# A count matrix built one chunk and one block at a time, in PSUM banks picked by registers, with W_in folded and the degrees summed from slabs

## The reference

```python
h = x @ W_in + b_in                        # x: relu(layernorm(x))
deg = segment_sum(ones, dst); deg = maximum(deg, 1.0)
for l in range(3):
    agg = segment_sum(h[src], dst) / deg
    h = relu(agg @ W_agg[l] + h @ W_self[l] + b_hid[l])
return h @ W_out + b_out
```

## Time and profile before

| | us |
|---|---|
| median of 3 runs | 7475.61 |
| lowest and highest | 7471.18, 7477.4 |
| profiled execution, span | 7482.7 |
| PE, DVE, ACT, POOL busy | 6524.4, 3687.6, 2350.1, 3090.6 |
| mean granted clock of PE | 0.929 of 2.4 GHz |

### The profile page before, as it was taken

How to read it: one execution, slowest core, us unless ns; L and a number is a source line. 1 busy time by engine, 2 the same in 40 slices (tenths; PEclk the granted TensorE clock), 3 DMA queues, 4 the chain that set the end, 5 groups by cost and what they waited for, 6 DMA issues and landing times.

```text
span 7482.7 us, 126299 instructions
## 1 busy us (share of the span) xinstructions
PE 6524.4 (87%) x29550; PEld 4866.3 (65%) x29551; DVE 3687.6 (49%) x10588; ACT 2350.1 (31%) x6423; POOL 3090.6 (41%) x3455
## 2 busy tenths in 40 slices
PE   5888888999999999998888987599999997777777
PEld 2333333788877878776666666477778886666666
DVE  9999999111111112224777777612223333555554
ACT  6888887000000001112222221312223333222222
POOL 5777776000100011114777775200011111777775
PEclk9999999999999999998877777799999998899898
DMA  5555557877987797775333333688897775444443
GB/s 194 211 215 211 214 213 250 316 273 274 336 292 272 280 339 260 253 255 173 101 99 99 99 99 103 234 324 290 294 357 245 249 246 188 119 122 121 121 123 95
DMA packets 668862, 1601.14 MB, mean 214 GB/s; under 512 B 77659, under 2 KB 306989, under 8 KB 668605
## 3 DMA queue, kind: packets, MB, share of 16 engines
q1 hardware_dynamic: 543133, 1232.09, 46.5%
q0 software_dynamic: 125488, 365.75, 16.1%
HBM read 1208.17 MB, written 390.27 MB: 214 GB/s over the span
## 4 chain that ended last, share of the span: by engine, by line
PE 51%; POOL 11%; issue 7%; DMA 7%; DVE 4%; ACT 1%; DVEq 1%; SPq 0%; POOLq 0%; ACTq 0%
PE psum L1343 35%; POOL ring L1096 6%; PE psum L1192 4%; PE psum L1619 3%; POOL tbuf L1096 3%; PE psum L1591 2%; DMA g_own<-own_dram 2%; POOL rb L1096 2%; DMA slab<-adj 2%; PE psum L1603 1%; PE psum L1522 1%; PE psum L1187 1%; PE psum L1292 1%; PE psum L1301 1%; DMA tbuf<-rel_table,idx_slot 1%
## 5 line engine op out<-in xcount | busy, mean ns | idle before, releaser
L1343 PE MATMUL psum<-X,slab 128*128 128x512 f32 x12495 | 3104.2, 402 | 87.8 <-DMA slab<-adj 43.7
L1343 PEld LDWEIGHTS psum<-X,slab 128*128 128x128 f32 x12495 | 2345.2, 190 | 618.7 <-DVE g_x L2336 89.3
L2486 DVE TENSOR_TENSOR acc<-acc,psum 128x264 f32 (+1 forms) x1660 | 704.2, 424 | 508.1 <-PE psum L1619 369.1
L1008 POOL DMA_DIRECT2D table<-s_tab x147 | 80.2, 545 | 1905.2 <-DVE s_tab L2083 1905.2
L974 POOL TENSOR_SCALAR hot_j<-iota_j,col_now 128x392 bf16<-128x392 bf16 x587 | 783.3, 1346 | 0.0
L1464 PE MATMUL psum<-hot_j,hot_key 128*128 128x392 bf16 x2348 | 583.6, 330 | 190.5 <-DVE hot_j L2299 149.0
L2313 DVE SCALAR_TENSOR_TENSOR staged<-staged,keep_all,psum 128x392 fp32r<-128x392 f32 x1174 | 717.0, 611 | 7.6 <-PE psum L1464 5.2
L1706 ACT ACTIVATE key_sq<-iota_row,edge_key 128x128 f32<-128x128 f32 x2055 | 657.4, 389 | 2.3 <-DVE staged L2288 2.3
L2083 DVE TENSOR_TENSOR s_tab<-psum,s_tab 128x256 fp32r<-128x256 f32 x196 | 82.7, 422 | 1141.5 <-ACT s_tab L1663 1141.5
L2299 DVE TENSOR_SCALAR hot_j<-iota_j,edge_col 128x392 bf16<-128x392 bf16 x1761 | 567.3, 349 | 0.0
L1658 ACT COPY s_hT<-psum 128x256 f32<-128x256 f32 x273 | 101.7, 373 | 1349.2 <-PE psum L1187 1349.2
(11 more groups left out here) (417 smaller groups left out, 8822.3 us busy)
## 6 DMA issues: line engine op xcount, KB each, us to landing
slab<-adj SPq DMA_DIRECT2D x385, 1344.0 KB, 6.5
slab<-adj SPq DMA_DIRECT2D x315, 896.0 KB, 5.9
adj<-staged SPq DMA_DIRECT2D x1174, 196.0 KB, 1.9
X<-table SPq DMA_DIRECT2D x33, 1792.0 KB, 13.0
table<-s_tab POOLq DMA_DIRECT2D x147, 256.0 KB, 3.1
g_own<-own_dram POOLq DMA_DIRECT2D x35, 896.0 KB, 8.4
own_dram<-s_out POOLq DMA_DIRECT2D x147, 128.0 KB, 5.5
acc<-zero_rows SPq DMA_DIRECT2D x2, 6600.0 KB, 27.4
```

The source lines that it names most:

```text
L1343: last = nc.tensor.matmul(sums_of(j), slab[:, slab_at(c), u, j * P:(j + 1) * P], X[:, x_at(p, d), :], start=(d == 0), stop=(d == KT - 1))
L2486: V.tensor_tensor(a, a, psum[:, bank, 0:w], ALU.add).then_inc(sem("summed"), 1)
```

## The change

The chunks are now single (782 of 128 edges), a step is the meeting of one chunk with one block, and a block with many chunks is cut after every 32: 1592 steps, 808 parts. PE accumulates a part in one bank of a ring of four, picked by a register z (its running number + 1), and clears the next bank with a two-column matmul in each step, after waiting until it has been evicted. ACT evicts each part once, when the step count of its end, read from a register, is reached; SP stores it. DVE makes all hot columns and the even keys, POOL the odd ones. Where z and the ends come from: DVE computes them at the start, POOL scatters the ends by 13 indirect DMAs (parts_dram), SP reads them back. x is loaded whole (49 tiles) and its statistics are taken before the build. W_in is multiplied into the agg and self weights by PE at the start, its bias likewise. The degrees: DVE adds up all rows of each group's slabs one group ahead, PE turns the sum into columns with seven one-column matmuls, and SP waits for DVE (slab_summed) too before it fills a slab's buffer. Early slabs and rows of pass 0 are issued by POOL.

```diff
-    C2 = C // 2
-    MEETS = C2 + BLOCKS - 1
-    PART = 16
-    BUILD = 24
+    PART = 32
+    CUTS = (C - 1) // PART
+    ENDED = BLOCKS + CUTS
+    RING = 4
+    LEAD = RING - 1
+    BUILD = 32
+    HOT, KEYS = 16, 32
+    NOW = 16
+    MEETS = -(-(C + BLOCKS - 1 + CUTS) // AT_ONCE) * AT_ONCE
...
             def slab_in(p, k, c, i=None):
                     sp.wait_ge(*ev("slab_done", at if i is None else i * NC + at))
+                    if p == 0 or p == 1 and k == 0 and c < SLABS:
+                        sp.wait_ge(*ev("slab_summed", at if i is None else i * NC + at))
...
+            def parts_out(i):
+                sp.load(to_regs, part_to[0:1, bass.ds(i * AT_ONCE, AT_ONCE)])
+                for r in range(AT_ONCE):
+                    sp.wait_ge(*ev("evicted", i * AT_ONCE + (LEAD + r + 1)))
+                    to = sp.snap(to_regs[r], min_val=0, max_val=PARTS + MORE - 1)
...
+            for s in range(SB2):
+                nc.gpsimd.indirect_dma_start(
+                    out=parts_dram, out_offset=bass.IndirectOffsetOnAxis(ap=at_i[:, s:s + 1], axis=0),
+                    in_=part_out[:, s, :], in_offset=None).then_inc(sem("parts_stored"), 16)
...
+            def group_degrees(slabs):
+                def f(t0):
+                    pe.wait_ge(*ev("slab_summed", slabs))
+                    pe.wait_ge(*ev("l0_own", t0 + 1))
+                    for j in range(GT):
+                        last = nc.tensor.matmul(PS_DEG[:, j:j + 1], slab_sum[:, j * P:(j + 1) * P], ones[:, 0:1], start=True, stop=True)
+                    last.then_inc(sem("l0_degrees"), GT)
...
+            def cleared(bank_ap):
+                nc.tensor.matmul(bank_ap, iota_k[:], iota_k[:, 0:2], start=True, stop=True, skip_group_check=True)
             def build(t, steps):
                 for s in range(steps):
                     beside(in_stages, t, s)
-                    for h in range(2):
-                        last = nc.tensor.matmul(psum[:, s % 4, 0:J], hot_key[:, s // 2 % 4, s % 2, h, :], ...
-                    last.then_inc(sem("meet_mm"), 1)
-                    if not static or n >= 2:
-                        degrees(t, s - 2)
+                    if s % AT_ONCE == 0:
+                        pe.load(zs, step_part[0:1, bass.ds(t * BUILD + s, AT_ONCE)])
+                    z = pe.snap(zs[s % AT_ONCE], min_val=1, max_val=LEAD + ENDED)
+                    if s % 4 == 0:
+                        pe.wait_ge(*ev("hot", t * BUILD + (s + 4)))
+                        pe.wait_ge(*ev("hot_odd", t * (BUILD // 2) + (s // 2 + 2)))
+                    own = (z & (RING - 1)).with_bounds(min_val=0, max_val=RING - 1)
+                    nc.tensor.matmul(psum[:, bass.ds(own, 1), 0:J].rearrange("p o j -> p (o j)"), hot_key[:, s % KEYS, :], hot_j[:, s % HOT, :],
+                                     start=False, stop=True, skip_group_check=True).then_inc(sem("meet_mm"), 1)
+                    pe.wait_ge(sem("evicted"), z)
+                    next_own = ((z + 1) & (RING - 1)).with_bounds(min_val=0, max_val=RING - 1)
+                    cleared(psum[:, bass.ds(next_own, 1), J:J + 2].rearrange("p o j -> p (o j)"))
...
+            def parts_evicted(i):
+                act.load(last_regs, part_last[0:1, bass.ds(i * AT_ONCE, AT_ONCE)])
+                for r in range(AT_ONCE):
+                    act.wait_ge(sem("meet_mm"), act.snap(last_regs[r], min_val=1, max_val=MEETS))
+                    if not isinstance(i, int):
+                        act.wait_ge(*ev(f"staged_out{r}", i * 16))
+                    nc.scalar.copy(staged[:, r, :], psum[:, (r + 1) % RING, 0:J]).then_inc(sem("evicted"), 1)
...
+            dve.wait_ge(*ev("in_x", 16 * X_LOADS))
+            for t in range(T):
+                last = V.bn_stats(x_st[:, t, :], x_all[:, t, :])
...
             def hot_columns(s):
+                if s % 2 == 0:
+                    V.tensor_scalar(hot_key[:, s % KEYS, :], iota_k[:], edge_now[:, 1, s:s + 1], None, op0=ALU.is_equal)
+                V.tensor_scalar(hot_j[:, s % HOT, :], iota_j[:], edge_now[:, 0, s:s + 1], None, op0=ALU.is_equal).then_inc(sem("hot"), 1)
...
-                    V.scalar_tensor_tensor(out=staged[:, s % AT_ONCE, :], in0=staged[:, (s - 1) % AT_ONCE, :].bitcast(F32), ...
+            def slabs_summed(g, i, c):
+                for u in range(2 if c == 0 else 0, SIZES[c]):
+                    V.tensor_tensor(slab_sum, slab_sum, of[u], ALU.add).then_inc(sem("slab_summed" if u == SIZES[c] - 1 else "slab_partly"), 1)
...
+            dve.wait_ge(*ev("meet_mm", MEETS))
+            for c in range(NC):
+                slabs_summed(0, None, c)
+                if c == 6:
+                    gathered_rows()
+                if c == 12:
+                    turn_tables()
```

More of the change, by code:

```diff
@@ L278, in build @@
         X_FIRST = 2
[L279 removed]
+        X_EARLY = 3
+        X_AT = [[n * GT for n in range(NG)],
                 [2 * GT, 3 * GT, 4 * GT, 5 * GT, 6 * GT, 0, GT]]
@@ L508, in tiles_of, with early @@
             return tile
+        EARLY = [(17, "rows", 0), (31, "rows", 1), (35, "slab", 0), (37, "slab", 1), (39, "slab", 2), (41, "slab", 3), (45, "rows", 2)]
+        def early(name, n):
+            return next(16 * (at + 1) for at, (_, *what) in enumerate(EARLY) if what == [name, n])
+        for n in range(SLABS):
+            shared[f"slab{n}"] = (f"slab_in{n}", -16)
         def x_in(p, b):
@@ new lines, in _ @@
+            last.then_inc(sem("in_WB"), 1)
+            pe.wait_ge(*ev("in_WT_read", 1))
+            for n, name in enumerate(("agg", "self")):
+                for q in range(Q):
+                    for b in range(Q):
+                        last = nc.tensor.matmul(PS_W[n][:, q * D:(q + 1) * D], s_u[:, b, q, :], cols(W["in", name], D)(b),
+                                                start=(b == 0), stop=(b == Q - 1))
+                last.then_inc(sem("in_W"), 1)
+            pe.wait_ge(*ev("bound", 1))
@@ L1486, in _ @@
+            by_meets(pe, build, 2)
+            pe.wait_ge(*ev("evicted", LEAD + ENDED))
             pe.wait_ge(*ev("in_own", T + 1))
@@ new lines, in _ @@
+            bounds_read(bounds_t, "bound_read")
+            once(V.tensor_scalar(to2, block, float(BLOCKS), float(MORE), op0=ALU.is_ge, op1=ALU.mult))
+            once(V.tensor_tensor(to2, to2, block, ALU.add))
+            once(V.tensor_scalar(other, to2, -1.0, float(BLOCKS - 1), op0=ALU.mult, op1=ALU.add))
+            once(V.tensor_tensor(other, other, cuts, ALU.mult))
+            once(V.tensor_tensor(to2, to2, other, ALU.add))
+            once(V.tensor_scalar(at2, step, float(ELSEWHERE), None, op0=ALU.add))
@@ L2193, in _ @@
+            once(V.tensor_tensor(at2, at2, upto, ALU.add))
+            V.tensor_copy(at_i, at2)
+            once(V.scalar_tensor_tensor(out=code, in0=code, scalar=before[:, 0:1], in1=cuts, op0=ALU.add, op1=ALU.mult))
             once(V.tensor_tensor(to2, to2, code, ALU.add))
+            V.tensor_copy(part_out[:, :, 0], to2)
+            V.tensor_scalar(part_out[:, :, 1], step, 1.0, None, op0=ALU.add).then_inc(sem("parts_out"), 1)
             once(V.tensor_scalar(code, code, 1.0, None, op0=ALU.subtract))
```

780 lines of the change are left out of this document (384 added, 396 removed), and 2 rows, old and new, of the table TILE_EVENTS.

## The result

The changed kernel takes 7602.18 us (median of 4 runs, 7597.29 to 7607.17) where the kernel before takes 7476.5: a ratio of 1.0166, 95% interval 1.0152 to 1.0181. It is slower by about 125 us. They stand in four places: the first matmul of the build comes 15.5 us later, the build is 71.5 us longer, pass 0 is 29.6 us longer, and all the rest is 6 us.

The account below looks back on a forecast made before the run. It took PE's own queue of register operations to bound the new build, where DVE had bound the old. Terms of 37 + 12 + 24 = +73 us on 7475.6 gave 7549 us, with a range of 7340 to 7680.

Parts of the forecast that it names:

- the likeliest case: Build on PE: six register operations a step, step 0.77 to 0.83 us, total 7500 to 7630; chance 0.46.
- The queue bounds the build: Build: PE's register operations, 0.106 us each and six a step, set the pace; the other engines cost nothing beside PE.
- Term 1: Build: 1592 steps of 0.796 us give 1267 us against 1230 before, +37 us.
- Term 2: Start, DVE's chain before the first step: +12 us, mostly the layer norm's statistics of 49 tiles, about +18.
- Term 3: Pass 0, slab sums on DVE and one-column products on PE: +24 us, from +10 to +70.
- one-column products: Pass 0: seven more PE products per group for the degrees, 1.4 us a group, 10 us in all.
- The ring of slabs: Pass 0: a slab is freed only when DVE and PE have read it; 1 to 1.5 us per group, 9 us.
- The first group: Pass 0: DVE waits for the last edge transposes with slabs unsummed, about 5 us for PE.
- The rest: The other passes and both edge stages stay as they were.
- Five operations a step: Build: copy of z free or one mask fused; step 0.690, build 1098 us, total 7380; chance 0.26.
- The queue free of bounds and DVE at 0.42: Build: PE's queue isn't the bound, DVE's 0.42 us is the step; build 669, total 6950; chance 0.05.
- Loads by SP's price: Build: register loads cost PE what SP pays, 0.20 us more a step, total 7860; dearer load or wait, chance 0.08.

Follow-up runs that it names:

- load_four: Changed kernel with TensorE loading four registers every fourth step in place of eight every eighth: 7630.4 us in one run.
- short_stats: Changed kernel with the 49 statistics at the start reading 16 of 256 columns: 7601.63 us in one run.
- two experiments on pass 0: Changed kernel with, in one, DVE's slab sums cut to 8 columns (7615.65 us); in the other, one PE degree product per group in place of seven (7593.8 us).
- act_zeroed: Changed kernel without clearing matmuls: ScalarE zeroes each bank after copying it out, and PE has two register operations a step; ratio 0.9678 to the kernel before.
- narrow_columns: Changed kernel with VectorE's hot columns compared over 8 columns in place of 392 in the loop's turns: 7609.04 us in one run.
- wide_clear: Changed kernel with each step's clearing matmul writing 120 columns in place of 2: 7617.11 us, ratio 1.0173 to the kernel before.
- short_sums: Changed kernel with VectorE's slab sums in pass 0 adding 8 columns in place of 896 from each group's third row on: 7615.65 us.
- one_degree: Changed kernel with TensorE making one one-column product per group of pass 0 in place of seven: 7593.8 us.
- seven_ops: Changed kernel with one mask more in each step, seven register operations in place of six: 7748.88 us in one run.
- five_ops: Changed kernel without the copy of z into a second register, five register operations a step in place of six: 7507.48 us.
- four_ops: Changed kernel with both banks packed into the loaded word, so four register operations a step and no copy: 7387.57 us, ratio 0.9877 to the kernel before.
- four_ops_wide: The kernel of four_ops with the clearing matmul widened from 2 to 120 columns: ratio 0.9833 to the kernel before.
- zero_narrow: The kernel of act_zeroed with ScalarE zeroing 8 columns of a part's bank in place of 392: 7143.28 us in one run.

## Why the prediction was right, and where its terms were off

The direction, and the mechanism of the likeliest case, held; 7549 was forecast and 7602 measured, inside the range and inside the narrower 7500 to 7630 of the likeliest case. The three terms and the rest all erred the same way, by 34.5, 3.5, 5.6 and 6 us. Point by point:

**The queue bounds the build: shown.** Six operations, each 0.106 forecast and 0.087 to 0.104 found (without the 0.03 of a matmul, which the forecast had in it); 0.636 forecast for a plain step, 0.64 found. Adding one costs 161 us, leaving one or two out gives 86 and 206. DVE, ACT, SP and POOL were rightly costed at nothing.

**Term 1 was +71.5, not +37; what was mis-sized is the load.** The prediction took 0.35 us for a load of eight registers from a row of four words in 0.332. The row was right (load_four repeats it at 0.333), but eight are 0.593 at the median and 0.72 on the mean, up to 2.11, and the next operation starts 0.06 after a load's end: 0.78 from start to start. Why 82 of the 199 last longer than 0.61 is open; a queue still full of matmuls isn't the reason, for the load at 613.21 us lasts 1.09 although the last matmul before it ended 0.05 us after its start. With its address a load is 0.106 a step where 0.057 stood: 0.049 x 1592 = 78 us. Two smaller errors took nearly as much off, 0.044 a step or 70 us: the waits of every fourth step cost 0.024, since one of the two is carried by the mask and needs no instruction, and not 0.053; loop and layer 0.035 and not 0.05. The six operations with their matmuls are 0.654 over all steps and not 0.636, 29 us more. Sum 0.819, measured 0.818. That term 1 was off by only 34 us is in part luck.

**Term 2 was +15.5, not +12.** The statistics took 16.1 us of DVE (18 forecast) and short_stats shows them on the path. 2.4 us of it came back at the end of the build, where the degree sums no longer follow the last matmul (pass 0 starts 0.6 us after it, before 3.0).

**Term 3 was +29.6, not +24, and for other reasons; that the size is near is luck.** The ten microseconds of one-column products were right as busy time: 12.4 in groups 1 to 6. The ring of slabs, 9 us forecast, never held PE. In its place DVE's stage operations came late behind the sums, 9.6 us. The first group, where 5 us of loss were forecast, is 4.5 us shorter (98.2 to 93.7). And 9.3 us are two pauses that nothing of before showed; see below. Over groups 1 to 6 the sum is 12.4 + 9.3 + 8.4 (waits for s_out, less 1.2 for s_h before) + 6.2 (row matmuls, 528.1 against 521.9) - 1.9 (waits for g_x) = 34.4, measured 34.2. This is a reading of one trace: why the row matmuls are 6.2 us busier wasn't looked for, and the two experiments on pass 0 say that its terms don't add freely. A group of before lasts 98 us there (588.4 / 6), not the 90 that the prediction took from a window of 90 us that it named a group; no number hung on it but the margin of the slabs.

**The rest** was forecast to stay and moved by 8.5 us: pass 1 by -1.6, pass 2 with the attention +4.5, pass 3 -1.1, and the fifth pass with what follows +6.7. This last stood between +5 and +12 in every profile of the changed kernel and its variants on the usual chips; its cause wasn't looked for.

**The rivals.** Five operations a step was forecast at 7380 and is 7507 when built: its break-even of 0.750 a step was nearly met (0.764). The forecast took the whole step for queue time, while the eleven places around the layer's products don't shrink, and 376 waits need an instruction of their own. The queue free of bounds and DVE at 0.42: only act_zeroed comes near, 0.44 in its first 160 steps. Loads by SP's price: too dear threefold.

## What to carry to other kernels

Work that only a queue does (masks, copies, addresses, loads of registers) is bound by count, about 0.1 us each on this PE, and shows as "issue" while every engine looks half idle: count these operations per step before trading VectorE's time for an address. Choose the word that is loaded so that each field needs one mask and the same instruction carries the wait. When the binding queue is shortened, look at once at which places of the turn the array or the next engine already held.

## What the runs showed of the hardware beyond that

**Pauses at the turn of a loop, and the transfers of instructions beside them.** Timeline of PE where the loop of pass 0 turns for the first time, changed kernel:

```profile
1689.90 0.95 PE L1373 MATMUL psum<-X,slab 128*128 128x512 f32 x3 [1.73 <-DVE g_x L2390]
1695.58 1.87 PE L1373 MATMUL psum<-X,slab 128*128 128x512 f32 x4 [4.73 <-issue]
```

Two such pauses, 9.3 us, stand in the changed kernel, and they recur (8.2 to 10.3 us) in the five variants whose PE program is as long ahead of that loop (narrow_columns, wide_clear, short_sums, short_stats, one_degree). None over 1.8 us stands in those where it is longer or shorter there (seven_ops, load_four, five_ops, four_ops, four_ops_wide, act_zeroed, zero_narrow). The code of the pass is the same in all but one_degree. The loop's branch, and the queue that carries instructions in the 15 us after it, in the changed kernel (1684 to 1699 us) and in load_four (1725 to 1740):

```profile
L1385 PEldq COMPARE_BRANCH  x15: 76/3522/7083, 1684.0 to 6397.3; - x15
```

```profile
q8 instruction: 3, 0.05, 1.3%
```

```profile
q8 instruction: 2, 0.03, 0.8%
```

A branch that is taken in pass 0 lasts 5.4 to 7.2 us in every trace, before's too, and the one that isn't taken 0.08 (the branch of the build's loop, also taken, is followed by the next operation after 0.28); a transfer of 16 KB on the instruction queue stands inside each that is taken. The matmuls already queued cover part of it. The first idle time at each turn (the 1.73 us above) ends 0.3 us after the branch does, so it is the branch's, although it is put down to DVE. A second such transfer follows in every trace, and at each of the twelve pauses of the six kernels PE goes on 1.3 to 1.6 us after the end of it. A rule of the Trainium skill (Runtime: NRT & Kernel Launch, Instruction fetch mechanics) says as much: a taken branch to code outside the window held makes the engine wait for a transfer. The traces agree with it. That the place of the code decides whether the second transfer comes too late is argued from the lengths of the programs; no run moved the code alone.

**The granted clock differed between the builds, the queue's pace didn't.** The clock was 1.00 before, 0.57 changed, 0.63 with the wider clear, 0.62 with four operations, 0.78 with both; the spacing of register operations was 0.09 to 0.11 us at all of them.
